# Layer 0's rows stored early, and the last addition of a two-block kernel moved from VectorE into GpSimd's accumulating stores

## What is computed

```
x  = L0_attn_x
xn = layernorm(x);  s = linear_attention(xn);  g = silu(experts_0(xn));  x = x + s * g     # layer 0
xn = layernorm(x);  s = test_time_training(xn); g = silu(experts_1(xn)); x = x + s * g     # layer 1
return x
```

## Time and profile before

| what | value |
|---|---|
| median of 3 runs | 453.63 us (453.40 to 454.32) |
| the profiled execution | 454.52 us |
| its span, first to last instruction | 452.8 us |
| TensorE busy / VectorE / ScalarE / GpSimd | 92% / 63% / 47% / 34% of the span |
| mean granted TensorE clock | 0.975 of full |

### The profile page before, as it was taken

The page is one execution under the profiler, slowest core; times in us unless marked ns, Lnnn a source line. Parts: engine busy times, 40 slices in busy tenths (PEclk is TensorE's granted clock), DMA queues, the critical chain, the costliest instruction groups (busy, mean ns, idle before and its releaser), DMA issues.

```text
span 452.8 us, 9800 instructions
## 1 busy us (share of the span) xinstructions
PE 414.3 (92%) x2920; PEld 349.0 (77%) x2920; DVE 285.4 (63%) x1137; ACT 213.5 (47%) x525; POOL 154.5 (34%) x215
## 2 busy tenths in 40 slices
PE   6689989999999999998898999889999999899883
PEld 6568876787869779787766879678899899799721
DVE  2489888987888878888857577413334344244417
ACT  3155546484544645544424443313555555555512
POOL 6150005213213450334333012453355555545510
PEclk9699999999999999999999999979999999999997
DMA  7419711235173321131213123411122222222577
GB/s 184 113 38 189 106 28 35 66 92 187 36 207 95 97 53 38 44 83 52 76 52 80 44 51 89 141 37 41 55 70 71 72 70 71 72 64 72 152 267 212
DMA packets 63426, 40.80 MB, mean 90 GB/s; under 512 B 18324, under 2 KB 56088, under 8 KB 63384
## 3 DMA queue, kind: packets, MB, share of 16 engines
q1 hardware_dynamic: 58688, 31.27, 27.9%
q0 software_dynamic: 4352, 8.99, 6.0%
q10 hardware_dynamic: 344, 0.03, 0.1%
HBM read 21.78 MB, written 18.48 MB: 89 GB/s over the span
## 4 chain that ended last, share of the span: by engine, by line
PE 48%; issue 20%; DVE 15%; DMA 6%; ACT 4%; SPq 2%; POOL 2%; DVEq 2%; POOLq 0%; ACTq 0%
PE psB L851 6%; PE psB L839 5%; PE psA L1025 5%; PE psB L1048 3%; DMA x_all<-in_L_attn_x_dram 2%; PE psC L1037 2%; PE psD L968 1%; DMA ring<-routed 1%; DMA routed<-send,slot 1%; PE psC L742 1%; PE psA L802 1%; DVE stats L1321 1%; PE psD L1005 1%; PE psA L797 1%; DVE x_all L1663 1%
## 5 line engine op out<-in xcount | busy, mean ns | idle before, releaser
L690 POOL DMA_INDIRECT routed<-send,slot x64 | 63.4, 991 | 127.0 <-DMA routed<-send,slot 56.2
L699 POOL DMA_INDIRECT results<-nat,y_to x72 | 69.9, 971 | 94.0 <-DVE nat L1634 77.3
L1025 PE MATMUL psA<-xuT,w_all 128*128 128x256 f32 x288 | 69.0, 382 | 2.1 <-issue 1.2
L1235 ACT ACTIVATE h1T<-psA,b1T 128x256 f32<-128x256 f32 x144 | 62.4, 473 | 17.5 <-PE psB L1048 13.8
L1025 PEld LDWEIGHTS psA<-xuT,w_all 128*128 128x128 f32 x288 | 50.5, 190 | 10.3 <-issue 2.2
L1037 PE MATMUL psC<-w_all,h1T 128*128 128x128 f32 x464 | 56.8, 276 | 1.1 <-DVE nat L1618 1.1
L1037 PEld LDWEIGHTS psC<-w_all,h1T 128*128 128x128 f32 x464 | 54.1, 192 | 1.7 <-issue 1.7
L1606 DVE TENSOR_SCALAR xu<-ring 128x256 f32 (+1 forms) x38 | 11.7, 307 | 68.4 <-DMA ring<-routed 64.2
L1226 ACT ACTIVATE xuT<-psB 128x256 f32<-128x256 f32 x37 | 14.2, 383 | 60.4 <-PE psB L1015 33.9
L839 PE MATMUL psB<-xnT,w_l 128*128 128x512 f32 x64 | 34.6, 622 | 0.0
L851 PE MATMUL psB<-w_l,hg0T 128*128 128x128 f32 x256 | 32.7, 281 | 0.2 <-ACT hg0T L1166 0.2
(11 more groups left out here) (289 smaller groups left out, 868.2 us busy)
## 6 DMA issues: line engine op xcount, KB each, us to landing
ring<-routed SPq DMA_DIRECT2D x38, 130.0 KB
inv<-inv_room SPq DMA_DIRECT2D x8, 512.0 KB, 4.1
w_all<-results SPq DMA_DIRECT2D x15, 256.0 KB, 4.7
routed<-ring SPq DMA_DIRECT2D x24, 130.0 KB, 6.6
n_room<-nT SPq DMA_DIRECT2D x8, 256.0 KB
w_all<-in_L_ffn_W_dram SPq DMA_DIRECT2D x1, 2048.0 KB
out_dram<-x_all SPq DMA_DIRECT2D x8, 256.0 KB, 2.3
results<-nat,y_to POOLq DMA_INDIRECT x72
```

The source lines that it names most:

```text
L690: pool.indirect_dma_start(routed[:, :], bass.IndirectOffsetOnAxis(ap=slot[par][:, c, t:t + 1], axis=0), send[par][:, c, t, :], None).then_ ...
L699: pool.indirect_dma_start(results[:, :], bass.IndirectOffsetOnAxis(ap=y_to[:, par, a:a + 1], axis=0), yw[:, par, a, :], None).then_inc(S[f ...
L1025: last = mm(psA[:, j // 2, (j % 2) * UNIT:(j % 2 + 1) * UNIT], w1_all[:, e, j * P:(j + 1) * P], xuT[:, :], start=True, stop=True)
L1235: f(h1T[:, j, :], psA[:, j // 2, (j % 2) * UNIT:(j % 2 + 1) * UNIT], ACT.Gelu, bias=b1T[:, n:n + 1]).then_inc(S["gelu_ready"], 1)
```

## The change

```
+                    elif k == FIRST_ALL - 2:
+
+                        wait_on(sp, "x1_ready", groups)
+                        for g in range(groups):
+                            sp.dma_start(out_rows[:, g * TILES:(g + 1) * TILES, :],
+                                         x_all[:, g * TILES:(g + 1) * TILES, :]).then_inc(x_stored, 16)
                     load_unit(k, k % E * REGION + k // E * UNIT)
...
             load_results(1, res_higher, res_in)
-            for g in range(groups):
-                sp.wait_ge(S["x2_ready"], g + 1)
-                sp.dma_start(out_rows[:, g * TILES:(g + 1) * TILES, :],
-                             x_all[:, g * TILES:(g + 1) * TILES, :]).then_inc(S["x_out"], 16)
             sp.wait_ge(S["x_out"], 16 * groups)
...
             pool.sem_inc(all_landed, 1)
+
+            pool.wait_ge(x_stored, 16 * groups)
+            pool.sem_inc(apart, 1)
+            for g in range(groups):
+                pool.wait_ge(S["mix_ready"], g + 1)
+                pool.dma_start(out_rows[:, g * TILES:(g + 1) * TILES, :], x_all[:, g * TILES:(g + 1) * TILES, :],
+                               accum_op=ALU.add).then_inc(S["x_out"], 16)
...
             def finish(g):
                 ts = slice(g * TILES, (g + 1) * TILES)
-                m = mix2[g % 2][:, :, :]
                 dve.wait_ge(S["silu1_ready"], g + 1)
-                v.tensor_tensor(m, s1[:, ts, :], th1[g % 2][:, :, :], ALU.mult).then_inc(S["mix_ready"], 1)
-                dve.wait_ge(S["mix_ready"], g + 1)
-                v.tensor_tensor(x_all[:, ts, :], x_all[:, ts, :], m, ALU.add).then_inc(S["x2_ready"], 1)
-
+                v.tensor_tensor(x_all[:, ts, :], s1[:, ts, :], th1[g % 2][:, :, :], ALU.mult
+                                ).then_inc(S["mix_ready"], 1)
+
+            dve.wait_ge(x_stored, 16 * groups)
+            dve.sem_inc(apart, 1)
             dve.wait_ge(S["s1_ready"], groups)
```

More of the change, by code:

```diff
@@ L302, in two_block_kernel @@
         th1 = [hg0T[:, i, :].rearrange("p (t d) -> p t d", t=TILES) for i in range(2)]
-        mix2 = [hg0T[:, 2 + i, :].rearrange("p (t d) -> p t d", t=TILES) for i in range(2)]
         res_lower = [w1_all[:, g, :].rearrange("p (a d) -> p a d", d=D) for g in range(groups - 1)] + [nT[0][:, :, :]]
@@ L352, in two_block_kernel @@
         all_landed = sem("all_landed")
+        x_stored = sem("x_stored")
         lower_in = [sem(f"lower_in{g}") for g in range(groups)]
@@ L384, in two_block_kernel @@
             "y_landed",
-            "sum_ps", "mix_ready", "silu1_ready", "x2_ready", "x_out",
+            "sum_ps", "mix_ready", "silu1_ready", "x_out",
         )}
```

## The result

| | before | changed |
|---|---|---|
| median | 453.51 us (451.65 to 454.32, 4 runs) | 464.11 us (462.47 to 465.61, 4 runs) |
| ratio | | 1.0243, 95% interval 1.0197 to 1.0289 |
| profiled execution, its span | 454.52 us, 452.8 us | 462.47 us, 460.7 us |

The change costs 10.6 us by the medians and 11.0 by the ratio, which goes by all runs of each kernel. The two profiled executions differ by 7.9 us only, because before's is slower than all four of its runs in the table and the changed kernel's is the fastest of its four. Runs scatter more than the 0.3% named at the start: on one chip, 23 runs of the kernel before took 449.3 to 454.2 us.

The account below looks back on a forecast made before the run. VectorE was taken to bound the last 11 us. To the profiled 454.5 us came 3.0 (queue), 2.0 (clock) and 4.6 (accumulating stores), 464.1, or 463.2 us on the median's scale; range 453.2 to 476.

Parts of the forecast that it names:

- The queue, 3.0 us: At unit 6's load: early stores ahead in SyncE's queue delay it, so unit 3's results start 3.0 us later.
- unit 6 isn't held: Rival at unit 6's load: early stores get through in time or cost the chain nothing; 458.2 us, chance 0.12.
- The clock, 2.0 us: TensorE after the longer wait for unit 6: its clock falls to half, losing 2.0 us.
- VectorE's additions removed: At the end: eight additions leave VectorE, so the last product ends 3.5 us before the last addition did.
- The accumulating stores, 4.6 us: At the end: GpSimd's eight adding stores land last at 457.1 instead of 452.4, 4.6 us later.
- a second stream: At the end: each piece stored with addition is also read from memory by the same engines, 14.2 us of data.
- a free addition: Rival at the end: adding costs no data time, 7.2 us of data, GpSimd's pace rules; 458.9 us, chance 0.15.
- GpSimd's pace, 1.27 us per store: At the end: GpSimd issues one store per 1.27 us, so the eighth starts at 449.7.
- GpSimd pays per piece: Rival at the end: a row of 512 pieces takes GpSimd 3.88 us; 482 us, chance 0.14.
- The faster rival: Rival at the end: adding stores cost no more than SyncE's, the last product sets the end, 450.2 for 452.4; chance 0.09.

Follow-up runs that it names:

- Kernel 8: Kernel before plus the early stores, four ahead of unit 6's load and four behind unit 7's; ratio 1.0017 to the kernel before.
- kernel 2: Changed kernel with the eight early stores moved behind unit 7's load; ratio 1.0139 to the kernel before.
- kernel 1: Kernel before with only the eight early stores added, ahead of unit 6's load; ratio 1.0099 to the kernel before.
- Kernel 4: Kernel before without VectorE's additions, SyncE storing the products alone; ratio 0.9905 to the kernel before.
- kernel 3: As kernel 2, but GpSimd's last stores are plain, so the output holds the products alone; ratio 1.0024 to the kernel before.
- kernel 7: As kernel 2, but both stores of a group go to a scratch buffer in 2 KB pieces instead of 512 bytes; ratio 1.0139 to the kernel before.
- kernel 5: Kernel before plus one 2 KB GpSimd store to a scratch buffer after the eighth addition; ratio 1.0107 to the kernel before.
- kernel 6: Kernel before plus one 2 KB GpSimd store to a scratch buffer after the fourth addition; ratio 0.9987 to the kernel before.
- kernel 9: Kernel before with the additions of groups 1, 3 and 5 made by GpSimd instead of VectorE; ratio 1.0041 to the kernel before.
- kernel 10: Kernel before with the change made for groups 2 and 3 alone; ratio 0.9993 to the kernel before.

## Why the prediction was right, step by step

The forecast was 463.2 us and 464.1 was measured. Its terms held unequally.

**The queue, 3.0 us: right.** Unit 3's results were expected at 288.45 and started at 288.23. The stores ran in the queue's order, as said, but faster than the 291 GB/s that I took (329 from 280 to 285, by the transfer records), and unit 6's first packet moved at 286.0 instead of 287.0; its own packets then took some 1.2 us instead of 0.5, the last of the stores' still moving beside them (until 286.8). The two errors nearly cancel. SyncE's room was too small as well: its eight issues took 6.92 us, not 3.2, so unit 6's load was issued 2.3 us later, but the queue was later still. Kernel 8 shows what the term is: not a price per byte, but the part of the bytes that exceeds the slack. The rival "unit 6 isn't held" would have been right for half the stores. Its sum, 4.6 us more than before, has the end without the drain; kernel 2, where unit 6 isn't held, cost 6.3.

**The clock, 2.0 us: the fall was there, its price is not isolated.** The clock falls to the 1.2 GHz level right behind the longer wait in both traces with eight stores ahead of unit 6's load (changed kernel, kernel 1); in the other ten it stays at 1.00 from 284 to 300. What was missing of the full clock there comes to 1.6 us in the changed kernel (0.50 and 0.71 over two windows of 2 us) and 1.7 in kernel 1 (0.53 over 2 us, 0.81 over 4), an estimate of what the fall can have cost. The runs agree: kernel 1's six have a mean granted clock of 0.977 where the kernel before has 0.982 beside them, some 2.3 us of full clock over the span, also an estimate. But before's own loss at 302 to 306 was absent in the changed kernel's trace; such a stretch behind 300 us stands in four of the twelve traces, with early stores and without. By difference, 10.6 less 3.0 for the queue and 6.8 for the tail leaves 0.8 us, and kernel 1's 4.5 less 3.0 leaves 1.5; both intervals take in 0 and 2.0. No kernel here separates the clock from the wait that comes before its fall.

**VectorE's additions removed: right.** The last product was expected to end 3.5 us before the last addition did. Against the start of the tail it came 3.3 us earlier (447.09 + 0.69 - 435.75 = 12.0 for 15.3). Kernel 4 turns that into a landing 2.7 us earlier.

**The accumulating stores, 4.6 us: right in size, for a reason that does not hold.** First row to landing was 16.2 us for 16.3 predicted, and the landing moved by 4.0 us against the tail's start. By the transfer records the data flowed from 443.34 to 457.13, 13.8 us for the 14.2 of a second stream and the 7.2 of a free addition. The choice between these was made by the transfer share of 1.00, read as engines with no time left. That reading is wrong: the earlier trace rows has a 1.05 itself, the early stores ran at a share of 1.14 and the accumulating ones at up to 1.44. So it was partly luck that the choice came out. What bears the second stream out are kernels 2, 3 and 7: 256 GB/s without the addition, 174 with it, and little more with longer pieces. Against kernel 3 the rate is 0.68, and VectorE's products paced that kernel's stores, one per 0.86 us; against SyncE's early stores of the same rows, 329 GB/s, it is 0.53, near the doubling. Of the 16.2 us, 2.0 pass before the first data, 2.10 MB at 174 GB/s are 12.0, and most of the rest is a slower start, 141 and 155 GB/s at 444 to 448, which I had not foreseen. Kernel 7 has it too (135 and 128 at 440 to 444), and its cause stays open. The sentence from the Trainium skill's "Collectives: The Full Stack", section on the bandwidth ceiling, that a reduction reads two sources agrees in kind with that; the one in its stop on SDMA and CCE that the addition is free stands there beside two reads and a write, and a store that adds at the price of a plain one, as the rival had it, is shown by no kernel here.

**GpSimd's pace, 1.27 us per store: right in size, without consequence.** It was taken from indirect stores. The rows of the stores that add overlap: each waits behind the one ahead, and their lengths of 1.4 to 3.1 us count that wait. The first, the shortest with 1.38, ends at 442.71 and the eighth at 451.87, seven steps of 1.31 us; that is what GpSimd needs for one. Plain rows took 0.75 us (kernel 3), rows that add in 2 KB pieces 0.87 to 1.05 (kernel 7). The data, 1.5 us per store at 174 GB/s, is slower than 1.31, so the pace is not the bound. The rival in which GpSimd pays per piece, 3.88 us for a row (482 us), falls. The Trainium skill's "DMA: Bandwidth & Descriptors", section on the anatomy of a DMA from GpSimd, says that many descriptors can be emitted before their cost shows; the rows agree in that 512 pieces are far from 3.88 us, but a quarter of the pieces (kernel 7) does shorten them.

**The drain, 2.8 us: missed.** The sum ended with the landing. The kernel before's trace had the row, 5.30 us at 434.8, hidden by 12 us of other work, and I didn't ask what would hide it once GpSimd's last work came last. With the 2.8 the predicted tail term is 7.4 instead of 4.6. The total came out near all the same: the landing was put 0.6 us too late, and the clock's 2.0 were counted in full where 0.8 are left by difference. So the mechanism of the end was incomplete, and that 463.2 is so close to 464.1 is partly luck.

**The faster rival: its condition failed.** It asked for over 220 GB/s. Plain GpSimd stores pass that (250 to 262), accumulating ones don't. Even a free addition would have left the tail 1.0 us longer than before (19.1 against 18.1), for the drain alone.

## What to carry to other kernels

Before work is moved to another engine at a program's end, look up that engine's own closing rows in the trace and ask what hides them: here the end waits until some 5.4 us after GpSimd's last instruction, or some 3 us after its last landing, whichever is later. An addition in a store is not free where the stores are the bound: count a second stream of bytes. Extra transfers in front of a load that is waited for cost nothing up to the slack that the queue has there and everything beyond it, so split them over several gaps.

## What the runs showed of the hardware beyond that

- GpSimd's closing drain ended 5.3 to 5.4 us after its last instruction where nothing was outstanding any more or a 2 KB store was (kernels 5, 6, 9; in the kernel before its row is 5.30 us), and 2.8 to 3.0 us after the landing where that was later (the changed kernel, kernels 2, 3, 7, 10). A DRAIN row's start can lie before the end of GpSimd's last rows, so its length alone (5.3 to 12.1 us) tells little; its end does.
- GpSimd's eight accumulating stores made 4224 packets for 2.10 MB, 4096 of them of 512 bytes; as plain stores (kernel 3) they made 640, 512 of them of 4096 bytes, by the transfer records. The rates were 174 and 256 GB/s, and one row took 1.31 and 0.75 us of GpSimd.
- A transfer share of 1.00 in a window is no ceiling: the early stores stood at 1.13 to 1.15 with 343 to 350 GB/s (280 to 286, changed kernel), stores that add at 1.41 to 1.44 with 171 to 178 (448 to 456).
- VectorE and GpSimd exclude each other in operations of two inputs each (kernel 9): 1.64 us instead of 0.69 for the one that meets the other.
- SyncE's issue of a 256 KB store took 0.37 us at the end, where one came per 1.3 us, and 0.47 to 1.17 us where eight followed each other (line 550, changed kernel), so a store that nobody waits for can hold the loads behind it twice, on the queue and on the engine.
